# Each filtered layer as one program, with its row transforms in another order

## The reference

```python
x = x + _L0_conv_ref(_gn(x), L0_conv_h0, L0_conv_numerators, L0_conv_denumerator)
x = x + _L1_conv_ref(...)      # patch mixer
x = x + _L2_conv_ref(...)      # 3x3 convolution
x = x + _L3_conv_ref(_gn(x), L3_conv_h0, L3_conv_numerators, L3_conv_denumerator)

def _L0_conv_ref(x, h0, numerators, denumerator):      # _L3_conv_ref is the same
    a = jnp.pad(denumerator, ..., constant_values=1.0)
    b = jnp.pad(numerators, ..., constant_values=0.0)
    h = irfft2(rfft2(b, s=(128, 128)) / rfft2(a, s=(128, 128)))
    H_full = h0 + rfft2(h, s=(256, 256))[0]
    X = jnp.fft.rfft2(x, s=(256, 256), axes=(-3, -2))
    Y = jnp.einsum('...hwi,ijhw->...hwj', X, H_full)
    return irfft2(Y, s=(256, 256))[..., :128, :128, :]
```

## Time and profile before

| | |
|---|---|
| median of three runs | 3530.05 us |
| the profiled execution's span | 3535.8 us |
| mean granted TensorE clock over the span | 0.968 |
| busy: PE, PEld, ACT, DVE, POOL | 92%, 76%, 48%, 44%, 36% |
| DMA, mean over the span | 121 GB/s |
| first filtered layer, with its barriers | 637.8 to 1178.8 us |
| last filtered layer | 2996.5 us to the end |

### The profile page before, as it was taken

How to read it: one execution, slowest core, us unless ns; L and a number is a source line. 1 busy time by engine, 2 the same in 40 slices (tenths; PEclk the granted TensorE clock), 3 DMA queues, 4 the chain that set the end, 5 groups by cost and what they waited for, 6 DMA issues and landing times. The chain is left out here.

```text
span 3535.8 us, 82659 instructions
## 1 busy us (share of the span) xinstructions
PE 3239.9 (92%) x37272; PEld 2671.5 (76%) x37272; DVE 1570.7 (44%) x1926; ACT 1681.8 (48%) x1763; POOL 1257.6 (36%) x1018
## 2 busy tenths in 40 slices
PE   7999999589998699999899999999989978799996
PEld 6999998289997576666687776666678754499996
DVE  6788876411111434444765543343764454311111
ACT  3666665356553344444554434444454431455650
POOL 6888885055552102222540001222280000255550
PEclk9999999799999899999999999999999988899998
DMA  0333333877775521222133332121222353867765
GB/s 18 115 120 121 121 115 132 223 210 198 195 191 126 147 95 61 82 72 82 61 108 100 109 113 76 67 95 48 86 81 60 95 157 55 200 193 193 196 184 154
DMA packets 259193, 429.38 MB, mean 121 GB/s; under 512 B 27479, under 2 KB 105817, under 8 KB 257369
## 3 DMA queue, kind: packets, MB, share of 16 engines
q1 hardware_dynamic: 244746, 398.80, 38.8%
q10 hardware_dynamic: 14096, 25.31, 2.2%
HBM read 306.59 MB, written 114.29 MB: 119 GB/s over the span
## 5 line engine op out<-in xcount | busy, mean ns | idle before, releaser
L138 PE MATMUL m_bank<-xn,w 128*128 128x512 f32 x1536 | 618.3, 403 | 31.9 <-DVE m_store L1563 11.7
L139 PE MATMUL m_bank<-xn,w 128*128 128x512 f32 x1536 | 602.5, 392 | 0.0
L140 PE MATMUL m_bank<-xn,w 128*128 128x512 f32 x1536 | 601.9, 392 | 0.0
L802 PE MATMUL c_acc<-c_shifted,filt 128*32 128x224 f32 (+8 forms) x11264 | 455.4, 316 | 30.9 <-DMA c_shifted<-spectrum_dram 27.7
L802 PEld LDWEIGHTS c_acc<-c_shifted,filt 128*32 128x32 f32 x11264 | 441.8, 159 | 38.7 <-DMA c_shifted<-spectrum_dram 29.3
L581 ACT ACTIVATE filt<-filt 64x2048 f32<-64x2048 f32 (+3 forms) x256 | 424.7, 1758 | 20.4 <-PEq L18 11.0
L568 POOL TENSOR_TENSOR filt<-filt 64x1408 f32<-64x1408 f32 x64 | 259.5, 4055 | 486.8 <-DMA filt<-filters_dram 486.8
L129 ACT ACTIVATE w<-raw_weights 128x2048 fp32r<-128x2048 f32 x96 | 372.9, 3884 | 102.8 <-PE m_bank L140 101.5
L138 PEld LDWEIGHTS m_bank<-xn,w 128*128 128x128 f32 x1536 | 290.9, 189 | 173.1 <-issue 76.4
L133 DVE TENSOR_TENSOR w<-raw_weights,w 128x2048 fp32r<-128x2048 f32 x86 | 333.3, 3875 | 159.2 <-ACT w L129 159.2
L140 PEld LDWEIGHTS m_bank<-xn,w 128*128 128x128 f32 x1536 | 290.8, 189 | 62.9
(11 more groups left out here) (179 smaller groups left out, 6766.6 us busy)
## 6 DMA issues: line engine op xcount, KB each, us to landing
c_shifted<-spectrum_dram SPq DMA_DIRECT2D x256, 270.0 KB, 3.9
filters_dram<-f_stage SPq DMA_DIRECT2D x128, 512.0 KB, 3.5
filt<-filters_dram SPq DMA_DIRECT2D x240, 256.0 KB, 4.6
raw_weights<-in_L_conv_Wq SPq DMA_DIRECT2D x16, 2048.0 KB, 8.6
raw_weights<-in_L_conv_Wk SPq DMA_DIRECT2D x16, 2048.0 KB, 8.5
raw_weights<-in_L_conv_Wv SPq DMA_DIRECT2D x16, 2048.0 KB, 8.6
m_qf<-in_L_conv_Wout SPq DMA_DIRECT2D x128, 256.0 KB, 3.8
spectrum_dram<-s_rows SPq DMA_DIRECT2D x128, 136.0 KB, 2.4
```

The source lines that it names most:

```text
L138: pe.matmul(out, w[0], x[0], start=first, stop=False)
L139: pe.matmul(out, w[0], x[1], start=False, stop=False)
L140: return pe.matmul(out, w[1], x[0], start=False, stop=last)
L802: mm = nc.tensor.matmul(acc[k % 2][phase][32 * s:32 * s + 32, 0:B, LAGS * kb:HALF], filt[:, k, phase, :, :, 4 * kb + s].rearrange("p j c - ...
```

## The change

The three functions become one, `filtered_layer`, with one set of semaphores and no barrier within it.

- The row transforms run in the order of `ROW_ORDER`: all sixteen channels for the even frequencies, then all sixteen for the odd ones. Transposes follow the even ones.
- Each row block is stored by one DMA of all 128 partitions (`row_block`), where it was two of 64. The destination's access pattern is written by hand: 2 x 64 x 544.
- After the 22nd store SP loads the rows of group 0, and after the last store those of group 1. PE begins group 0 when the last row transform is through. `cols` lies in the spare buffer, the four row buffers in the ring place of group 3.
- In the last batch of four groups, SP loads the products of groups 0 to 27 into the places of the filter ring that are free (`load_products`). Those of the last four groups are moved on the chip, from `out` to `prod`, by eight DMAs whose destination is four partitions each (`move_products`).
- PE does three units' even halves right after the last group, and then the rest.
- The table of the inverse transform is loaded at the layer's start.

```diff
+    ROW_ORDER = [(par, i) for par in range(2) for i in range(C)]
+    LAST_EVEN = max(v for v, (par, i) in enumerate(ROW_ORDER) if par == 0)
+    FIRST_LOAD_AT = LAST_EVEN + 6
+        rows = shifted[:, RING - 1]
+        prod = filt[:].rearrange("p k h j c n -> p (k h j c n)")[:, 0:2 * C * B * L].rearrange("p (o j n) -> p o j n", o=2, j=C)
+        def row_block(i, par):
+            at = scratch["spectrum"][:, i, par * FW:(par + 1) * FW]
+            return bass.AP(tensor=at.tensor, offset=at.offset, ap=[[C * L * B * ROW, 2], [B * ROW, FW], [1, B * ROW]])
-            for u in range(2 * C):
-                i, par = u // 2, u % 2
-                sp.wait_ge(rows_ready, u + 1)
-                for part in range(2):
-                    sp.dma_start(scratch["spectrum"][part, i, par * FW:(par + 1) * FW],
-                                 rows[part * FW:(part + 1) * FW, u % 4].rearrange("p b q t -> p (b q t)")).then_inc(stored[u % 4], 16)
+            for v, (par, i) in enumerate(ROW_ORDER):
+                sp.wait_ge(rows_ready, v + 1)
+                sp.dma_start(row_block(i, par), rows[:, v % 4].rearrange("p b q t -> p (b q t)")).then_inc(rows_stored[v % 4], 16)
+                if v == FIRST_LOAD_AT:
+                    for k in range(4):
+                        sp.wait_ge(rows_stored[k], 16 * len(range(k, LAST_EVEN + 1, 4)))
+                    for s in range(4):
+                        load_rows(sp, 0, 0, s)
+            for s in range(4):
+                load_rows(sp, 1, 1, s)
             for k in range(4):
-                sp.wait_ge(stored[k], 16 * 2 * (2 * C // 4))
+                sp.wait_ge(rows_stored[k], 16 * (2 * C // 4))
...
+            def move_products(g):
+                k, f = g % RING, 4 * (g - GROUPS // 2)
+                for c in range(2):
+                    sp.dma_start(prod[FW * c + f:FW * c + f + 4, 1],
+                                 out[c:128:2, k].rearrange("p b t q -> p (b t q)")).then_inc(last_in, 16)
+            sp.wait_ge(progress, POINTS * (LAST_BATCH + 1))
+            for k in range(RING):
+                sp.wait_ge(prod_stored[k], 16 * (N_BATCHES - 1))
+            load_products(0, slice(0, FW), slice(0, 12), even_in)
+            sp.wait_ge(progress, POINTS * (LAST_BATCH + 2))
+            load_products(0, slice(0, FW), slice(12, 16), even_in)
+            load_products(1, SETTLED, slice(0, 8), odd_in)
+            sp.wait_ge(progress, POINTS * (LAST_BATCH + 3))
+            load_products(1, SETTLED, slice(8, 16), odd_in)
+            for k in range(RING):
+                sp.wait_ge(acc_out, LAST_BATCH + k + 1)
+                move_products(LAST_BATCH + k)
...
+            for u in range(AHEAD):
+                back(u, 0)
+            pe.wait_ge(odd_in, 16 * 4)
+            pe.wait_ge(last_in, 16 * 2 * RING)
+            for u in range(AHEAD):
+                back(u, 1)
```

More of the change, by code:

```diff
@@ L582, in lower_columns, with filtered_layer @@
                           scale=1.0 if column else -1.0)
-def spectrum(nc, image, source, layer, filt, scratch, const, tag):
+def filtered_layer(nc, layer, image, source, spare, filt, scratch, const, out_dram, tag):
+    N_BATCHES = GROUPS // RING
+    RUN = B * ROW - LAGS
+    FAR_AT, FAR = 2 * LAGS * NEAR, L - 2 * LAGS * NEAR
+    POINTS, HALVES_DONE = 11, 6
+    SPREAD = (0, 1, 2, 3, 5, 6, 7, 8)
+    LAST_BATCH = RING * (N_BATCHES - 1)
+    QUARTERS = 4
+    UNITS = [(quarter, b) for quarter in range(QUARTERS) for b in range(B)]
+    AHEAD = 3
+    ROW_ORDER = [(par, i) for par in range(2) for i in range(C)]
+    LAST_EVEN = max(v for v, (par, i) in enumerate(ROW_ORDER) if par == 0)
+    FIRST_LOAD_AT = LAST_EVEN + 6
+    TURN_AT = {19: (slice(EVEN, SUM), 0), 22: (slice(EVEN, SUM), 1), 25: (slice(SUM, 3), 0), 28: (slice(SUM, 3), 1)}
     with ExitStack() as ctx:
@@ new lines, in _ @@
+            for k in range(4):
+                sp.wait_ge(rows_stored[k], 16 * (2 * C // 4))
+            for m in range(8):
+                if m:
+                    sp.wait_ge(progress, SPREAD[m])
+                piece(sp, 2, 2, m)
+                piece(sp, 3, 3, m)
+            for n in range(1, N_BATCHES):
+                for k in range(RING):
+                    for m in range(8):
+                        sp.wait_ge(progress, POINTS * (RING * (n - 1) + k + 1) + SPREAD[m])
+                        piece(sp, RING * n + k, k, m)
@@ new lines, in _, with sum_of_filters @@
+        @block.gpsimd
+        def _(pool):
+            def sum_of_filters(n, k):
+                pool.wait_ge(filt_in[k], 64 * (n + 1))
+                sum_filters(nc.gpsimd, filt, k).then_inc(filt_summed, 1)
+            for k in range(EARLY):
+                sum_of_filters(0, k)
+            pool.wait_ge(freq_ready, 2 * C)
+            for n in range(N_BATCHES):
+                for k in range(RING):
+                    if RING * n + k >= EARLY:
+                        sum_of_filters(n, k)
+                    pool.wait_ge(rows_in[k], 64 * (n + 1))
+                    at = shifted[:, k].rearrange("p s b q t -> p (s b) q t")
+                    nc.gpsimd.tensor_tensor(total[:, k], at[:, :, 0, 0:HALF], at[:, :, 1, 0:HALF], ALU.add).then_inc(rows_summed, 1)
@@ L1852, in build @@
         with filter_tensor(nc, "filt1") as filt:
-            spectrum(nc, image, None, 1, filt, scratch, const, "s3_")
             with nc.sbuf_tensor("spare", [128, 2, 8, 512], F32) as spare:
-                convolve(nc, 1, spare, filt, scratch, "c3_")
-        back_to_image(nc, image, out, scratch, const, "b3_")
+                filtered_layer(nc, 1, image, None, spare, filt, scratch, const, out, "c3_")
 INPUTS = {
```

393 lines of the change are left out of this document (167 added, 226 removed).

## The result

PE is TensorE, PEld its weight loads, ACT ScalarE, DVE VectorE, POOL GpSimd, and SP the queue of SyncE. The changed kernel takes 3820.3 us, median of 4 runs (3815.95 to 3830.3), beside 3531.15 us for the kernel before, now the median of four runs: ratio 1.080, 95% interval 1.074 to 1.085. The forecast was 3801 in a range of 3700 to 4060: slower, as forecast, 19 us above.

A forecast was written before the change was run, and what follows sets the result against it. PE was taken as the bound, busy for 92%, so only its waits could yield gains. Heads +259 us, layer ends +8 and product loads +4 gave +271 on the median of 3530: 3801 us, range 3700 to 4060.

The forecast's parts named there:

- Two engines for the new store: Row stores at a layer's head: DRAM side counts 2, so 2 of 16 engines carry each store; 32 blocks take 188 us.
- three DMAs of 65 rows: Constant loads in the first 14 us: 13 completions each, read as rows dealt in equal shares along the outer count.
- 0.092 us for a packet and 5.9 us for a block: Row stores at a layer's head: 64 packets on each of two engines, at the lower price, per row block.
- The rival with 0.150: Row stores on two engines with packets at the old 0.150 us: 119 us more per layer, 4039 us; chance 0.11.
- Group 2 at 876 and 130 us later: Head of each layer: group 2 starts at 876 and 3229 instead of 747 and 3099, +129 and +130 us.
- the same 6.7 us: Head of a layer: time by which group 2 started ahead of its c_odd in the kernel before.
- PE waiting before both: Sign in the changed profile, head of a layer: PE waits before group 1 and group 2 for c_shifted.
- Loads of products, +4 for both layers: Last three groups of each layer: 12.6 instead of 11.9 us each under DMA load, +4 us in all.
- Moves at 4.0 us, +8: End of each layer: eight moves at 4.0 us each, 58 us against 55.4 and 52.6, +8 us for both layers.
- The rivals with 16 engines: New store on 16 engines, -46 at the heads: 3445 us with quick moves (chance 0.12), 3496 with slow moves (0.08).
- The listed chances: Forecast 0.55, two engines with quick moves 0.14 or slow packets 0.11, sixteen engines 0.12 and 0.08, no difference 0.01.
- four cases: Totals listed beside the chances for the whole kernel: 3801, 3750, 4039, 3445 and 3496 us.

The follow-up runs named there:

- e1: Changed kernel with each row block stored by two DMAs of 64 partitions, as before, instead of one: 3559.6 us, ratio 1.007 to the kernel before.
- e2: Changed kernel with its single store's DRAM side dealt as 64 x 2 rows instead of 2 x 64: 3548.4 us, ratio 1.001 to the kernel before.
- e3: Kernel before with the single 2 x 64 store in place of its two, old order and separate programs kept: 3812.5 us, ratio 1.075.
- e8: e1 with each of the two stores' 64 rows dealt as 4 x 16 on the DRAM side: 3645.2 us, ratio 1.031 to the kernel before.
- e4: e2 with the product loads cut into 16 pieces of two channels, each behind a point of PE's progress: 3521.4 us, ratio 0.994 to the kernel before.
- e11: e4 with the eight moves cut into 32 of one partition, half issued by ScalarE's queue: 3510.8 us, ratio 0.991 to the kernel before.
- e7: Kernel before with a single store of 64 x 2 rows, old order and separate programs kept: 3526.4 us, ratio 0.997.
- e5: e2 with all product loads held until group 31 is done: 3592.2 us, ratio 1.015 to the kernel before.

## Why the prediction was right, by its steps

- **Two engines for the new store: right, and shown** by the packets in flight in the changed kernel, by the landings of each store, by e1, e2, e3 and by e8's dose. The step had been inferred from three DMAs of 65 rows. The rule of the Trainium skill quoted with it holds for counts of 2 and 4 on the DRAM side.
- **0.092 us for a packet and 5.9 us for a block:** 0.089 and 5.6 measured. The rival with 0.150 has fallen. A small number of engines isn't needed for the low price: e2's sixteen have 0.088 too, from 128 partitions.
- **Group 2 at 876 and 130 us later:** its c_odd at 882.83 less the same 6.7 us is 876.1; the two heads are +129.4 and +131.4 against +129 and +130. Two errors inside the step cancel. The last block landed by 847.9 (when SP goes on behind its wait), not 855. Group 1, not group 2's loads, was late then: it waited 20.7 us for its own rows, and group 2 followed it without a wait for rows or filters. The text had PE waiting before both. Most of what made group 2 late was the low clock at the start of group 1 (0.75 from 852 to 864 us) and pauses of PE on issue, 2.1 us in group 1 and 4.0 in group 2, none of which the text had. That the step ends 0.1 us beside the trace is therefore luck; that it ends near it is not, since the last block's landing, its main term, was 7 us off out of 188.
- **Loads of products, +4 for both layers: the step that failed.** They were priced at 0.7 us a group, the cost of ordinary DMA load, with no term for PE standing still for instructions. From c_odd of group 28 to the last group's end are 68.3 us in layer 1 where before had 41.6, and 69.0 against 41.8 in layer 2: +26.7 and +27.2. Pauses of PE on issue are 17.1 of the first, and a clock of 0.87 makes most of the rest. Spread out, the same loads cost some 3 us a layer (e4: 39.8 us between the c_odd of groups 28 and 31, before 36.4).
- **Moves at 4.0 us, +8: too slow, and the two errors offset each other.** The first ones ran near the forecast's rate (29 GB/s at 1272 to 1274 us, where 33 were taken), but together the eight ran at 51 GB/s, 2.6 us each, and had started 8 us before the last group's end, since that came late. PE went on 14.2 and 15.0 us after it, where 29 were forecast. From the last group to the end of the last addition are 43.6 and 44.2 us, where 58 were forecast and before had 55.4 and 52.6: -11.8 and -8.4.
- Both together are +33.6 where 12 were forecast: the loads +53.9 for +4, the moves -20.2 for +8. That errors of +50 and -28 offset each other is luck; it keeps the total near the forecast and is the main part of the 19 us by which the forecast was low. The -9.1 in the middle of layer 2 goes the other way; e3's same stretch is 327.1 and e1's 322.3, so it varies by some us between profiled executions, and what it is stays open.
- **The rivals with 16 engines** had 3445 and 3496. e2 is that case, and it ran 3548, outside both: its head gained 10.5 us in layer 1 (23 forecast), and the stretched groups took that back. With the loads paced it is 3521, and with faster moves, as far as they go, 3511 (e11, whose interval overlaps e4's).
- The listed chances add to 1.01, and the "four cases" are five; neither touches the forecast.

## What to carry to other kernels

Look at the count of a DMA's slowest dimension on either side, and make it large (64 here, not 2 or 4). Halving the number of stores by making that count 2 cost 130 us a layer, and reordering a table's columns gave all of it back at no price. Both counts can be read in the source before anything runs. A large load that is issued early "under" a compute stretch may hold back that stretch: give it out in pieces tied to the engine's progress, and read the engine's idle time put down to issue. A transfer into few partitions stayed slow however it was cut here (50 to 63 GB/s); put it where nothing that is waited for stands behind it.

## What the runs showed of the hardware that was not expected

- TensorE paused 2.2 to 5.3 us at a time in groups 29 to 31 under a queue of 1.5 MB DMAs, each time until a 16 KB instruction packet had landed. 1.2 to 1.7 us lie between that and its next instruction. Shorter and rarer pauses of this kind are in the kernel before as well, under loads of filters and rows.
- A packet of 2176 bytes from SBUF to DRAM, 16 engines busy, took 0.166 us in stores of 64 partitions (the kernel before, e1) and 0.088 to 0.089 in stores of 128 (e2, e7).
- Moves into four partitions on four engines ran at 29 GB/s with 0.33 us a packet at first and at 69 with 0.09 later, with the same share of busy engines.
- Packets of 2048 bytes into single partitions, 16 at a time, took 0.52 us each instead of 0.09 and moved 63 GB/s, against 50 for four at a time.
- The clock that was granted in the head (655 to 855 us) is 0.58 of full, near the lower level of 1.2 GHz, with PE busy for 85.5 of 200 us; a transform of 512 columns took 1.03 us there, 0.65 before.
- The profiled executions of e2, e5, e7 and e8 are 14 to 21 us above their medians. In the first three layer 2's head comes 11 to 19 us later after layer 1's end than before's 1928.4, in kernels that share nothing in between but the unchanged stages. The sources of this are open; the totals above are medians.
